# Packing eight heads for the output projection of two attentions, instead of four

## What is computed

```
attn = softmax(scores)                                   # [B, 16, S, keys]
out = einsum('bhqk,bhkd->bhqd', attn, v)                 # 16 heads of 16
out = out.transpose(0, 2, 1, 3).reshape(B, S, 256)
out = out @ w_out + b_out                                # the output projection
x = layernorm(x + out)
```

## Time and profile before

| | |
|---|---|
| Timed runs | 2462.32 us median of 3 (2461.2 to 2466.6) |
| Profiled execution | span 2470.6 us |
| PE | 2108.0 us busy (85%) |
| DVE | 1446.1 us (59%) |
| ACT | 1215.5 us (49%) |
| POOL | 767.3 us (31%) |
| 16 DMA engines, SP's queue | 26.2% |
| PE clock granted, mean | 0.947 of 2.4 GHz |

### The profile page before, as it was taken

How to read it: one execution, slowest core, us unless ns; L and a number is a source line. 1 busy time by engine, 2 the same in 40 slices (tenths; PEclk the granted TensorE clock), 3 DMA queues, 4 the chain that set the end, 5 groups by cost and what they waited for, 6 DMA issues and landing times. The chain is left out here.

```text
span 2470.6 us, 33295 instructions
## 1 busy us (share of the span) xinstructions
PE 2108.0 (85%) x11586; PEld 1180.7 (48%) x11586; DVE 1446.1 (59%) x2698; ACT 1215.5 (49%) x2773; POOL 767.3 (31%) x1082
## 2 busy tenths in 40 slices
PE   6778888888888869999999985889899977788886
PEld 3333344344343345565555554556566643445455
DVE  5565466455655146566787885494834344557555
ACT  2345534544444436565787771567642314354352
POOL 4250220221001020011454551384824222443333
PEclk8889999999999879999999998999999978899898
DMA  7425433343241020000110114010001156544321
GB/s 157 105 45 135 83 75 70 75 86 76 42 67 45 20 74 1 7 29 25 44 59 24 47 46 156 32 43 9 28 26 49 37 118 123 116 94 89 80 59 40
DMA packets 132520, 156.60 MB, mean 63 GB/s; under 512 B 36493, under 2 KB 102929, under 8 KB 132258
## 3 DMA queue, kind: packets, MB, share of 16 engines
q1 hardware_dynamic: 132354, 154.47, 26.2%
HBM read 107.55 MB, written 46.86 MB: 62 GB/s over the span
## 5 line engine op out<-in xcount | busy, mean ns | idle before, releaser
L530 ACT ACTIVATE pbuf_sb<-psB 128x512 f32<-128x512 f32 (+1 forms) x608 | 330.8, 573 | 343.5 <-PE psB L409 318.5
L716 DVE TENSOR_REDUCE negm_sb<-psA 128x1 f32<-128x768 f32 (+6 forms) x352 | 347.4, 1022 | 135.6 <-PE psA L397 132.9
L406 PE MATMUL psB<-qst_sb,kst_sb 99*128 99x512 bf16 (+3 forms) x768 | 237.0, 339 | 42.0 <-ACT pbuf_sb L530 34.1
L1257 ACT ACTIVATE pw_sb<-psA,nmx_sb 128x154 f32<-128x154 f32 x512 | 191.9, 389 | 133.5 <-DVE nmx_sb L1402 133.5
L395 PE MATMUL psA<-kst_sb,qst_sb 96*128 96x512 bf16 (+3 forms) x768 | 200.0, 339 | 40.9 <-DVE negm_sb L716 34.4
L423 PE MATMUL psO<-pbuf_sb,V_sb 128*32 128x512 f32 (+3 forms) x1536 | 170.3, 517 | 8.4 <-ACT OT_sb L516 7.1
L1402 DVE TENSOR_REDUCE nmx_sb<-psA 128x4 f32<-128x616 f32 x128 | 101.8, 796 | 125.3 <-PE psA L1026 125.0
L406 PEld LDWEIGHTS psB<-qst_sb,kst_sb 99*128 99x128 bf16 x768 | 75.2, 99 | 183.2 <-ACT pbuf_sb L530 145.9
L2801 ACT ACTIVATE pb_sb<-psB 128x512 f32<-128x512 f32 x160 | 92.8, 601 | 134.3 <-PE psB L2691 131.1
L2918 DVE TENSOR_REDUCE negm_sb<-psA 128x2 f32<-128x320 f32 x256 | 115.9, 480 | 70.8 <-PE psA L2681 66.1
L395 PEld LDWEIGHTS psA<-kst_sb,qst_sb 96*128 96x128 bf16 x768 | 60.9, 99 | 165.0 <-DVE negm_sb L716 100.7
(11 more groups left out here) (308 smaller groups left out, 4580.6 us busy)
## 6 DMA issues: line engine op xcount, KB each, us to landing
qst_sb<-parts_dram SPq DMA_DIRECT2D x192, 128.0 KB, 4.6
rden_sb<-dens_dram SPq DMA_DIRECT2D x128, 128.0 KB, 2.7
parts_dram<-parts_sb SPq DMA_DIRECT2D x32, 384.0 KB, 2.8
kst_sb<-parts_dram SPq DMA_DIRECT2D x96, 128.0 KB, 7.3
x_dram<-X_sb SPq DMA_DIRECT2D x64, 128.0 KB, 1.7
y_dram<-yw_sb SPq DMA_DIRECT2D x16, 512.0 KB, 2.8
Y_sb<-y_dram SPq DMA_DIRECT2D x16, 512.0 KB, 9.3
parts_dram<-partsb_sb SPq DMA_DIRECT2D x16, 384.0 KB, 3.0
```

Source lines behind the costliest of these rows:

```text
L406: last = nc.tensor.matmul(psB[:, k, at:at + hi - lo], kst[0:MAX_ROWS, gg % 3, h, i * P:(i + 1) * P], qst[0:MAX_ROWS, gg % 3, h, lo:hi], st ...
L530: nc.scalar.activation(pbuf[:, key % 2, heads[0]:heads[-1] + 1, lo:hi], psB[:, (nb.n - 1) % 2, 0:len(heads) * (hi - lo)] .rearrange("p (h ...
L716: nc.vector.tensor_reduce(out=negm[:, gg % 2, heads[0]:heads[-1] + 1, j], in_=psA[:, (na.n - 1) % 2, :].rearrange("p (h n) -> p h n", h=le ...
L1257: last = nc.scalar.activation(pw[:, m % 2, h, :], psA[:, m % 2, at:at + K], ACT.Exp, bias=nmx[:, m % 2, h:h + 1], accum_out=psx[:, m % 3, ...
```

## The change

OT gets two buffers in place of six, and a new tensor OTC of four buffers holds the packed values of a pair of groups: after the copy of group g, four DMAs inside SBUF move the 16 feature rows of each head to rows 64 (g % 2) + 16 h of OTC. The inverses are broadcast to the same 16 rows a head. POOL scales a pair at once, 128 full rows, when the second group of the pair is there. The weights are loaded by one DMA as [128, 2, 256]; the memsets go. A projection tile is two products. ACT's copy of group g waits for the moves and the store of denominators of group g - 2. The last stage is changed in the same way (OT1, OTC1); of it only the parts that differ are shown.

```diff
-    OTN = 6
+    OCN = 4
-    wo_a0 = sb("wo_a0", [P, G, D], F32, first_stage)
+    wo_a0 = sb("wo_a0", [P, KC, D], F32, first_stage)
-    OT = sb("OT", [P, OTN, S], F32, first_stage)
+    OT = sb("OT", [P, 2, S], F32, first_stage)
+    OTC = sb("OTC", [P, OCN, S], F32, first_stage)
...
             def reciprocals(gg):
                 sp.wait_ge(o_free, 2 * (gg + 1))
-                sp.dma_start(dens_dram[0], OT[HD:P:32, gg % OTN, :]).then_inc(dens_stored, 16)
+                sp.dma_start(dens_dram[0], OT[HD:P:32, gg % 2, :]).then_inc(dens_stored, 16)
+                if gg // 2 >= OCN:
+                    sp.wait_ge(var_ready, NT * ((gg // 2 - OCN) // KC + 1))
+                for h in range(4):
+                    at = 64 * (gg % 2) + HD * h
+                    sp.dma_start(OTC[at:at + HD, gg // 2 % OCN, :], OT[32 * h:32 * h + HD, gg % 2, :]).then_inc(ot_moved, 16)
                 sp.wait_ge(dens_stored, 16 * (gg + 1))
...
-                if gg > 0:
-                    sp.wait_ge(ot_scaled, gg)
+                if gg > 1:
+                    sp.wait_ge(ot_scaled, gg // 2)
                 for h in range(4):
-                    sp.dma_start(rden[32 * h:32 * h + 32, :],
-                                 dens_dram[1, h:h + 1, :].broadcast_to([32, S])).then_inc(inv_loaded, 16)
+                    at = 64 * (gg % 2) + HD * h
+                    sp.dma_start(rden[at:at + HD, :],
+                                 dens_dram[1, h:h + 1, :].broadcast_to([HD, S])).then_inc(inv_loaded, 16)
...
             def project_out(b, j):
                 if j == 0:
-                    pe.wait_ge(wo_loaded, 16 * 5)
-                    pe.wait_ge(ot_scaled, G * (b + 1))
+                    pe.wait_ge(wo_loaded, 16 * 2)
+                    pe.wait_ge(ot_scaled, KC * (b + 1))
                 k = slot_a()
-                gemm(psA[:, k, 0:D], lambda g: OT[:, (G * b + g) % OTN, j * P:(j + 1) * P], lambda g: wo_a0[:, g, :],
-                     G).then_inc(a_full, 1)
+                gemm(psA[:, k, 0:D], lambda c: OTC[:, (KC * b + c) % OCN, j * P:(j + 1) * P], lambda c: wo_a0[:, c, :],
+                     KC).then_inc(a_full, 1)
...
             def copy_out(gg, c):
                 act.wait_ge(pv_done, 8 * gg + 4 * c + 4)
-                if gg >= OTN:
-                    act.wait_ge(var_ready, NT * ((gg - OTN) // G + 1))
+                if gg >= 2:
+                    act.wait_ge(ot_moved, 64 * (gg - 1))
+                    act.wait_ge(dens_stored, 16 * (gg - 1))
...
+            def scale_values(pair):
+                pool.wait_ge(ot_moved, 128 * (pair + 1))
+                pool.wait_ge(inv_loaded, 128 * (pair + 1))
+                nc.gpsimd.tensor_tensor(OTC[:, pair % OCN, :], OTC[:, pair % OCN, :], rden[:, :], ALU.mult).then_inc(ot_scaled, 1)
+                pool.wait_ge(ot_scaled, pair + 1)
...
-            nc.gpsimd.memset(wo_a0[:, :, :], 0.0).then_inc(wo_zeroed, 1)
...
-                if k >= 2 and early_groups(k - 2) is not None:
-                    scale_values(early_groups(k - 2))
+                done = early_groups(k - 2) if k >= 2 else None
+                if done is not None and done % 2 == 1:
+                    scale_values(done // 2)
...
-                    if j == 7 and 0 <= gg - 3 < GROUPS:
-                        scale_values(gg - 3)
+                    if j == 7 and 0 <= gg - 3 < GROUPS and (gg - 3) % 2 == 1:
+                        scale_values((gg - 3) // 2)
```

More of the change, by code:

```diff
@@ L479, in _ @@
             pe.wait_ge(a_free, na.n)
-            for g in range(G - 1):
-                pe.wait_ge(ot_scaled, G * (B - 1) + g + 1)
-                for j in range(NT):
-                    nc.tensor.matmul(late_tile(psA, j), OT[:, (G * (B - 1) + g) % OTN, j * P:(j + 1) * P], wo_a0[:, g, :],
-                                     start=(g == 0 and j < 4), stop=False, skip_group_check=True)
-            pe.wait_ge(ot_scaled, G * B)
+            pe.wait_ge(ot_scaled, KC * B - 1)
+            for j in range(NT):
+                nc.tensor.matmul(late_tile(psA, j), OTC[:, (KC * B - 2) % OCN, j * P:(j + 1) * P], wo_a0[:, 0, :],
+                                 start=(j < 4), stop=False, skip_group_check=True)
+            pe.wait_ge(ot_scaled, KC * B)
             for j in range(NT):
@@ L490, in _ @@
                     pe.wait_ge(a_free, na.n - 4)
[L491 removed]
+                nc.tensor.matmul(late_tile(psA, j), OTC[:, (KC * B - 1) % OCN, j * P:(j + 1) * P], wo_a0[:, 1, :],
                                  start=False, stop=True, skip_group_check=True).then_inc(a_full, 1)
@@ L2601, in reciprocals @@
                 sp.wait_ge(o_free, 2 * (gi + 1))
-                sp.dma_start(dens_dram[0], OT1[HD:P:32, gi % OTN, :]).then_inc(dens_stored, 16)
+                sp.dma_start(dens_dram[0], OT1[HD:P:32, gi % 2, :]).then_inc(dens_stored, 16)
+                if gi // 2 >= OCN:
+                    sp.wait_ge(zc_full, ZC_SLOT[("o", (gi // 2 - OCN) // KC, NT - 1)])
+                for h in range(4):
+                    at = 64 * (gi % 2) + HD * h
+                    sp.dma_start(OTC1[at:at + HD, gi // 2 % OCN, :], OT1[32 * h:32 * h + HD, gi % 2, :]).then_inc(ot_moved, 16)
                 sp.wait_ge(dens_stored, 16 * (gi + 1))
@@ L2861, in _, with scale_values @@
         def _(pool):
-            def scale_values(gi):
-                pool.wait_ge(inv_loaded, 64 * (gi + 1))
+            def scale_values(pair):
+                pool.wait_ge(ot_moved, 128 * (pair + 1))
+                pool.wait_ge(inv_loaded, 128 * (pair + 1))
                 for n in range(4):
                     at = slice(n * 256, (n + 1) * 256)
-                    last = nc.gpsimd.tensor_tensor(OT1[:, gi % OTN, at], OT1[:, gi % OTN, at], rden1[:, at], ALU.mult)
+                    last = nc.gpsimd.tensor_tensor(OTC1[:, pair % OCN, at], OTC1[:, pair % OCN, at], rden1[:, at], ALU.mult)
                 last.then_inc(ot_scaled, 1)
```

58 lines of the change are left out of this document (24 added, 34 removed).

## The result

Timed, the changed kernel takes 2425.7 us (median of 4 runs, 2422.9 to 2430.1) and the kernel before beside it 2463.6. The ratio is 0.9843, 95% interval 0.9827 to 0.986, some 38 us or 1.6%. In the four later comparisons, on other chips, the kernel before took 2470 to 2476; the changed kernel, timed again in one of them, had a ratio of 0.9829 (0.9794 to 0.9864). The forecast was 2421.5, a fall of 41.

A forecast was written before the change was run, and what follows sets the result against it. PE was taken to bound projection tiles in the first attention, DVE close behind in the last stage. Terms -20 + 1.5 - 16.2 - 4.3 - 3.5 + 1.5 = -41.0 us from 2462.3 gave 2421.3, said as 2421.5; 8 in 10 for 2410 to 2442.

The forecast's parts named there:

- the last block: Last batch's projection tiles in the last stage: first residual 1.9 us sooner, seven others lose DVE's idle time; 4.3 us saved.
- the late tail: End of the first attention: moves' issue +0.4, landing +0.5, PE's last products at half clock +0.5; 1.5 us lost, bounds 0 and 3.
- Part 1: First attention: two products a tile instead of four save PE time in 24 tiles; 20 us, lower bound 12.
- Part 3: POOL scales once for two groups: 0 in the first attention, 3.5 us saved in the last stage, bounds 0 and 7.
- rival (b): Thinned steps let PE's clock fall, losing parts 1 and 2, about 2460 us; chance 0.07 including a missed wait.
- Part 2: Last stage, 32 tiles with two products: 5.4 us a block, 16.2 for three, plus 4.3 for the last batch's block.
- The place at 2213: Last stage: POOL's even-group scaling at 2213.11 delays the 1/deviation, DVE waits 3.93 us and PE 5.03; dropping it saves 2.7.
- Part 4: Added moves on SP's queue, mostly hidden by its wait: 1.5 us lost in the late tail, 1.5 in the last stage.
- Rival (c): Slower: the moves hold the denominators' round trip back, deciding from 8 us a group; 2480 us at 12; chance 0.05.
- Rival (a): DVE becomes the bound: half of part 1 (10) and only 7.8 of part 2 come, 2441 us; chance 0.15.
- The rule weighed there: Part 4: transfer rate goes by SBUF ports reached, so halved broadcasts land no sooner; the sum some 3 us smaller.

The follow-up runs named there:

- half_products: The kernel before with two of the four products of every projection tile left out in both places, no moves, POOL as before; 2443.7 us, ratio 0.9873.
- s4_only: The change in the last stage alone, the first attention left as in the kernel before; ratio to the kernel before 0.9902.
- skip_even: The kernel before without POOL's waits for and scalings of the even groups in both attentions, all four products kept, no moves; ratio 0.9931.
- no_moves: The kernel before with the edits of both half_products and skip_even: two products a tile, no even scalings, no moves or packed buffer; ratio 0.9836.
- scale_each4: The kernel after, with POOL in the last stage again waiting for each even group's broadcast, then doing four multiplications into scrap; ratio to before 0.9852.
- pool_wait0: The kernel after, with POOL in the first attention again waiting for group 0's broadcast between its weight passes; ratio to the kernel before 0.9827.
- moves_late: The kernel after, with each group's four moves issued behind the load of the denominators in both attentions; ratio to the kernel before 0.9814.

## Why the prediction was right, and where it was not

The time came out within 4.2 us of the forecast. Of its terms, the products in the first attention, the last block and the late tail were right; POOL's part in both places and the products in the rest of the last stage were not.

**Part 1, right in size.** Twenty us were forecast. The six periods with tiles sum to 304.4 to 307.2 in the four traces with the projection of before and to 282.8 to 286.0 in the eight with the new one: 305.9 against 284.7 in the mean, 21.2 less. half_products has 286.7, so it is the products.

**The fourth period, missed.** Part 3 said of POOL's scalings in the first attention: "POOL mostly idles there and DVE hardly waits for it, 0". That step failed. POOL's idle time at the scaling of group 0 was a wait for a DMA, in POOL's fixed order, 12.8 us long, and what it held back was not this scaling but the passes behind it. The price did stand in the trace, as one wait of 10.5 us of PE for DVE's maxima (the waits of PE up to 225 us: total, times, longest), where nothing pointed at POOL, and DVE counts as busy while it is held:

```profile
PE psA L395 <- DVE negm_sb L716: 17.8, 17, 10.5
```

The same view of the kernel after has 8.1 us in 18 times, the longest 0.9. With it POOL's part is worth some 9 us here (55.3 in the mean of four against 46.0).

This is also where a rule of the Trainium skill would have helped. Shown first: a cast held for 6.96 and 4.62 us until POOL's pass ends, a DVE operation with two inputs in SBUF held for 3.75 to 4.62, and DVE's maxima from PSUM, 1.22 us for 1024 columns beside such a pass and without it. The Trainium skill (SBUF — State Buffer, section "Who interferes with whom") says that VectorE and GpSimd share a port pair as an exclusive lock, held for a whole instruction, that casts and operations with two SBUF inputs can be shut out by it, and that reductions aren't. The traces agree on which operations are held and on the lock's length for the casts. The operations with two inputs were done earlier, after 4.62 of a pass's 7.09 us and after 3.75 of 5.37.

**What was given back in the first attention.** The nine other periods, in which PE has the same work in both kernels, sum to 440.9 us in the mean of four (436.4 to 445.6) and to 446.5 in the eight with the new projection (443.6 to 450.2). Of these 5.6 us, 3.5 are PE's busy time and 2.2 its idle time. Of one period, before and after:

```profile
270.08:319.44 49.36, 41.25 (x273) 16.58 (x274) 25.20 (x28) 26.51 (x48) 14.43 (x14) 1.00 0.37 78
265.09:318.36 53.27, 43.99 (x273) 17.36 (x273) 25.30 (x28) 26.51 (x48) 14.02 (x13) 0.94 0.38 72
```

The same 273 products take PE 41.25 us at a granted clock of 1.00 and 43.99 at 0.94. This is the direction of rival (b), at 5.6 of its some 38 us. That the thinner tiles cause it is not shown; the two ranges overlap, and s4_only, with the four products, has 445.6.

**The late tail, right.** Forecast +1.5. Its rows after the earlier trace rows:

```profile
822.24 3.72 PE L487 MATMUL psA<-wo_a_sb,OTC_sb 128*128 128x256 f32 x16
...
823.00 0.54 SPq L259 DMA_DIRECT2D dens_dram<-OT_sb  x1
...
823.59 2.41 SPq L264 DMA_DIRECT2D OTC_sb<-OT_sb  x4
...
826.04 0.58 SPq L266 DMA_DIRECT2D dens_sb<-dens_dram  x1
...
833.58 1.22 DVE L745 TENSOR_TENSOR OTC_sb<-OTC_sb,rden_sb 128x1024 f32<-128x1024 f32 x1 [5.08 <-DMA rden_sb<-dens_dram]
```

The 16 products before the last scaling take 3.7 us and leave PE idle, as forecast. From the store to DVE's scaling it is 10.58 us against 9.21 (in the mean of all traces 1.1 more, forecast 0.9), and from the scaling to L666's last residual (L662's before) it is 14.29 against 13.75, PE's last products having started at half clock (forecast +0.5). The whole tail, from the last transpose on, scatters by more than this: 61 to 73 us over the 14 traces, the longest at granted clocks of 0.69 and 0.72.

**Part 2, the last block right, the other three too large.** The blocks from PE's first tile to the last residual: the first 25.1 before and 24.4 after (means of three and seven traces), the second 25.1 and 20.4, the third 24.9 and 20.4, the last 16.2 and 11.7. Forecast were 5.4, 5.4, 5.4 and 4.3; measured are 0.7, 4.7, 4.5 and 4.5. In the first block the gain stops at a DMA. DVE's reciprocal of a group's denominators stands, in DVE's order, between the fifth and the sixth residual, and PE's scores wait for what DVE does behind it. Before, then after:

```profile
2153.01 0.35 DVE L2936 RECIPROCAL dens_sb<-dens_sb 128x32 f32<-128x32 f32 x1 [0.45 <-DMA dens_sb<-dens_dram]
```
```profile
2128.45 0.35 DVE L2945 RECIPROCAL dens_sb<-dens_sb 128x32 f32<-128x32 f32 x1 [3.42 <-DMA dens_sb<-dens_dram]
...
2130.20 0.31 PE L2690 MATMUL psA<-kst_sb,qst_sb 97*128 97x160 bf16 x2 [2.54 <-DVE negm_sb L2927]
```

In all 14 traces the reciprocal begins 18.6 to 20.0 us after the block's first product, however many products a tile has. DVE waits for that load 0.4 to 1.9 us where a tile has four products, and 3.2 to 5.1 where it has two, with moves or without. The forecast let DVE decide here, but counted its 0.4 us before the reciprocal as idle time that shorter products would give back; it was a wait for a DMA, and it grew. PE, busy 25.7 of 25.7 us in this block before, is busy 20.5 of 24.0 after, its clock 0.86 instead of 0.89. Of the 13.3 us that the blocks of half_products save, 8.1 arrive at the end of the stage. The rest returns in the stretches between the blocks, as in the one before the last block, skip_even against no_moves, whose code differs in the products alone:

```profile
2337.16:2389.77 52.61, 38.62 (x179) 20.71 (x178) 23.38 (x55) 26.58 (x49) 18.06 (x33) 0.95 0.24 71
```
```profile
2322.70:2378.62 55.92, 41.80 (x179) 21.85 (x180) 23.36 (x56) 26.59 (x49) 18.14 (x34) 0.90 0.25 72
```

The same 179 and 180 products take 38.6 and 41.8 us, at 0.95 and 0.90. So the term of 20.5 for the products of this stage (16.2 and 4.3) was mis-sized; it measured 8 (9 between skip_even and the mean of the six kernels with neither wait nor work, moves included). Where the rest returns differs (in half_products 3.7 us of it between the second and the third block), and that it is always the clock isn't shown.

**Part 3 in the last stage, right in place and forecast at a quarter of its size.** The place at 2213 went as forecast:

```profile
2184.99 0.22 POOL L2890 TENSOR_SCALAR std_sb<-mv_sb 128x1 f32<-128x1 f32 x1
...
2185.90 0.41 DVE L2982 TENSOR_SCALAR XE_sb<-XE_sb,mv_sb,rstd_sb 128x256 f32<-128x256 f32 x1 [1.20 <-POOL rstd_sb L2891]
...
2186.77 0.31 PE L2690 MATMUL psA<-kst_sb,qst_sb 97*128 97x160 bf16 x2 [1.49 <-DVE negm_sb L2927]
...
2186.92 1.06 PE L2715 MATMUL psO<-pb_sb,v1r_sb 128*128 128x512 f32 x2
```

The 1/deviation is there 2.7 us sooner and DVE waits 1.20 instead of 3.93. But the price of that place was more than the wait. DVE's operation took 1.23 us beside POOL's next work and takes 0.41 now. PE's idle time before it was 5.03 us and is 1.49. After the 5.03 us PE ran at half clock; the same two products before:

```profile
2218.68 1.99 PE L2706 MATMUL psO<-pb_sb,v1r_sb 128*128 128x512 f32 x2
```

1.99 us against 1.06. Together the place cost 5 us where 2.7 were put down, and the whole part is 12.8 by skip_even (10.5 by scale_each4, whose work is smaller; forecast 3.5, upper bound 7). Of that, some 7 to 9 us lie in the stretch from the first to the second block: 82.1, 86.6 and 83.3 us before, 75.0 to 77.3 in all nine kernels without the even scalings. The places of the other 4 weren't found one by one.

**Part 4, hidden for the most part, as said.** SP's wait is 1.7 us a group shorter in both stages, of 2.4 us that the issue takes; no_moves has no moves and is no faster. The expected 1.5 us in the last stage isn't there (-1 was its lower bound). A group of four moves does not hold the queue: the load of the denominators goes out 3.04 us after the store instead of 1.85 in the late tail. Rival (c), from 8 us on, is out. (Its time was a slip too high: with 60 us in place of both 1.5s it is 2478, not 2480.) Rival (a) is out in the first attention, where DVE still waits for PE in 15 of the 24 tiles and 21 us came. In the last stage it came true in size: it had 7.8 and 4.3 us for the products, and 8 were measured. DVE's residual waits there for PE before 11 tiles of 32 instead of 22, and in the first block DVE waits for the denominators. The halved broadcasts land after 2.2 us in the median, 2.6 before. The rule weighed there, of the Trainium skill (SBUF — State Buffer, section "Door 1: The DMA port swizzle"), would have had them land no sooner; these runs don't bear that out.

**The sum** was right because errors met, and that was luck. In the last stage the products were 12 us too high and POOL's part 7 to 9 too low. In the first attention POOL's 9 us were missing, and 5.6 were lost again in the other periods, mostly at a lower clock, which isn't shown to come from the change.

## What to carry over

An engine that "mostly idles" can be standing in order at one instruction. Before such a wait is costed at nothing, read what is queued behind it, and on what it will fall when it starts; DVE operations of 7 us where their kin take 0.2 are the mark of it, and they stand under busy, not under waits. Before an engine's idle time is counted as a gain, read what each of its waits is for: one of 0.45 us for a DMA grew to 3.4 when the work ahead of it got shorter. Price an idle gap of PE with what follows it at half clock: in one place 2.7 us of wait cost 5. And where the terms are checked by their sum alone, wrong ones can pass: four kernels, with neither part, each alone and both, priced these two.

## What the runs showed of the hardware

A GpSimd pass over 2048 columns held a VectorE cast of 32x128 until its own end: begun 0.2 us into the pass (before) it took 6.96 us, begun 2.5 us into it (pool_wait0) 4.62, alone 0.21. An operation with two SBUF inputs, begun together with such a pass, was let go earlier, after 4.62 of 7.09 us (half_products, s4_only) and 3.75 of 5.37 (before, pool_wait0). A maximum over 1024 columns of PSUM took 1.22 us beside GpSimd and without it. A 64 KB move inside SBUF, 16 rows to 16 rows, landed 2.3 us after its issue in the median when it was issued behind the load of the denominators (moves_late), and 6.9 us in the first attention and 3.4 in the last stage when it followed the loads of stacked queries and keys (after, at most 8.8). Its issue took SP 0.59 us, a broadcast's 0.42.
